# Layer 0's router products of a four-layer adaLN/MoE kernel: a moving operand of 56 columns, 48 of them zeros, in place of 8

## The chip, the cores and the metric

The kernel runs on one core of a Trainium2 chip. The metric is the device time of one execution in microseconds; a profile gives the span from the first to the last instruction of one execution, which is a little shorter.

## The reference

The input is x, 8 sequences of 128 tokens with 128 features. Four layers follow; each takes a conditioning step and then a mixture-of-experts step, and adds the result to x. The change touches the routing of the first conditioning step:

```python
# layer 0, conditioning: D = 128, E = 8 experts, K = 2, N = 8*128 tokens
tf = broadcast(t_emb)                                  # one vector per sequence
shared = silu(xf @ w1) * (xf @ w3) @ w2
s = sigmoid(concat([xf, tf], -1) @ router_W)           # router_W is 256 x 8
topk_idx = top_k(s + router_bias, K)
gates = s[topk_idx] / sum(s[topk_idx])
h = gelu(einsum('nc,ech->enh', xf, W1e))
routed = sum_e combine[n, e] * (h[e] @ W2e[e])
out = (shared + routed) / 3
```

A second mixture (squared ReLU) completes layer 0. Layer 1 has a GRU over 128 steps, layer 2 a low-rank product per sequence, layer 3 a recurrence with tanh; each is followed by a mixture of 8 or 12 experts. All of it is float32, much of it split in two parts of the PE's rounded float32 type.

## The kernel before, in words

The program is written per engine. Each engine has its own instruction stream in which the order is set by hand, and they meet at semaphores. The tokens are cut into four chunks of 256 columns (32 time steps of 8 sequences). The work of the layers is a list of slots, `UNITS`; in slot n TensorE projects unit n into the bank `U` (`project`), ScalarE applies the activation (`hidden`), TensorE multiplies unit n - 2 down into the bank `Y` (`down`), and VectorE adds the weighted result into `acc_a` or `acc_b` (`add_l0`, line 1015 the first one, line 803 the others). Units "C" are layer 0's conditioning step, "F" its mixture. From slot `GRU_SLOT` on the steps of layer 1's GRU are put between them, and later those of layer 3's recurrence.

The start goes like this. GpSimd makes the identity (lines 487 and 488), clears buffers, and makes masks (lines 491 to 511), signalling `zeros` and `consts`; `own` makes GpSimd wait for its own instruction. TensorE multiplies the identity with itself eight times (`keep_busy`, line 1385), turns x eight times into the banks `Y` (line 1394), from where VectorE copies it into `xT` (line 903; the profile calls this buffer `h`), and multiplies twice more. It projects the units of slots 0 and 1 (`l_w`), and then comes `router_c` (line 1398), called in slot 1. It waits for the first loads and for the constants, turns the conditioning input and two small tables into bank M[0], waits until VectorE has laid out the conditioning vectors (`cond_tok`), and makes the router's scores in M[1]: for each of the 8 tiles of 128 tokens, the tile of `xT` is the stationary operand and the 8 columns of `l0_rw` are moved; a ninth product does it for the conditioning. All `mm` calls are recorded at line 1364, and a float32 product stands in the trace as two records.

VectorE takes the scores in `scores_c` (line 924): it copies the ninth product's 8 columns to `okay` and adds them to the 64 of the tiles, into `score`. ScalarE makes the sigmoid (`sigmoid_c`), and `route_c` on VectorE finds the two best experts and the weights `comb_x` of the first chunk at once, in slot 2, and of the rest in slots 4 to 9, between the additions of `add_l0`.

Of the kernel before, what the change touches and what calls it, by code (L numbers as in the profile page):

```python
# [7 lines left out]
ALU = mybir.AluOpType  # L8
# [3 lines left out]
P = 128  # L12
B, T, D = 8, 128, 128
# [4 lines left out]
E = 8  # L18
# [19 lines left out]
L0_UNITS += [("F", i, CHUNKS - 1) for i in range(6)]  # L38
HOLD = 4
MID_SLOT = 7  # L40
REST_C = 4
GRU_SLOT = L0_UNITS.index(("F", 5, 0)) + 5

# [23 lines left out]
def unit(n):  # L67

    return UNITS[n] if 0 <= n < len(UNITS) else ("", 0, 0)
# [50 lines left out]
def x_late(n):  # L120

    names = [("mid", m) for m in range(3) if n == MID_SLOT + m // 2]
    names += [("zp", unit(n - 3)[2])] if unit(n - 3)[:2] == ("A", LU - 1) else []
# [27 lines left out]
def at(start, n):  # L151

    return slice(start, start + n)
# [19 lines left out]
def adaln_ffn_program(nc, a, out):  # L173
    with ExitStack() as ctx:
        def sb(name, shape, dtype=F32, scope=ctx):
            return scope.enter_context(nc.sbuf_tensor(name, shape, dtype))
# [4 lines left out]
        def psum(name):  # L181
            return ctx.enter_context(nc.psum_tensor(name, [P, 512], F32))

        def sem(name):
            return ctx.enter_context(nc.semaphore(name))
# [8 lines left out]
        rows = sb("rows", [1, 3 * E + 1])  # L194
        rnn_b = sb("rnn_b", [D, 1])
        cond = sb("cond", [B, D])
        l0_rw = sb("l0_rw", [P, 2, E])
        b2 = [sb(f"l{l}_b2", [P, D]) for l in (1, 2)]
        gate_w = sb("gate_w", [P, 2, E])
        l2_v = sb("l2_v", [P, B * R])  # L200
# [6 lines left out]
        cond_tok = sb("cond_tok", [D, P])  # L207
# [11 lines left out]
        xT = h3[:, B:]  # L219
# [53 lines left out]
        with ExitStack() as early:  # L273
# [33 lines left out]
        score = sb("score", [P, NG])  # L307
# [16 lines left out]
        okay = sb("okay", [P, E])  # L324
# [11 lines left out]
        M = [psum("M0"), psum("M1")]  # L336
# [12 lines left out]
        m_full, m_free = sem("m_full"), sem("m_free")  # L349
# [25 lines left out]
            (rows[:, E:2 * E], a["L1_ffn_gate_b"].unsqueeze(0)),  # L375
            (rows[:, 2 * E:3 * E], a["L2_ffn_gate_b"].unsqueeze(0)),
            (rows[:, 3 * E:], a["L1_ffn_temperature"].unsqueeze(0)),
            (l0_rw[:, :, :], a["L0_cond_router_W"].rearrange("(h d) e -> d h e", h=2)),
            (l0f_rw_in[:, :], a["L0_ffn_router_w"]),
        ]  # L380
        small_loads = [
# [38 lines left out]
        def bank_of(*name):  # L420

            return M[m_of(*name) % 2]
# [62 lines left out]
        def _(pool):  # L485
            own = OwnOrder(pool, pool_own)
# [2 lines left out]
                               base=0, pattern=[[-1, P]], channel_multiplier=1).then_inc(ident_made, 1)  # L489
            for t in (cond_pair, b2[0], b2[1], l3_b2):  # L490
                pool.memset(t[:, :], 0.0).then_inc(zeros, 1)
            own(pool.memset(rank_mask[:, :], 1.0 / (D * R)))
            own(pool.memset(earlier8[:, :, :], 1.0))
            own(pool.memset(earlier12[:, :, :], 1.0))
# [82 lines left out]
        def _(sc):  # L577
# [14 lines left out]
            def mid_copies(n):  # L592
                if n == MID_SLOT + 1:
                    m = bank_of("mid", 0)
                    sc.wait_ge(m_full, m_of("mid", 0) + 1)
                    nc.scalar.activation(l2_uT[:, :], m[:, 0:P], ACT.Copy)
                    nc.scalar.activation(l2_wT[:, :], m[:, P:2 * P], ACT.Copy).then_inc(m_free, 1)
                if n == MID_SLOT + 2:
                    m = bank_of("mid", 2)
                    sc.wait_ge(m_full, m_of("mid", 2) + 1)  # L600
                    sc.wait_ge(m_free, m_of("mid", 1) + 1)
                    nc.scalar.activation(b1T[:, :], m[:, 0:2 * E * Q], ACT.Copy)
                    nc.scalar.activation(l3_pT[:, :], m[:, 128:128 + DA], ACT.Copy)
                    nc.scalar.activation(l3_uT[:, :], m[0:DA, 256:256 + NR3 * E3], ACT.Copy).then_inc(m_free, 1)
# [149 lines left out]
            def idle(*_):  # L754
                pass
# [34 lines left out]
        def _(dve):  # L790
            own = OwnOrder(dve, dve_own)
            v = nc.vector

            def tt(out, in0, in1, op):
                return v.tensor_tensor(out=out, in0=in0, in1=in1, op=op)  # L795
# [9 lines left out]
            def grp(t, g, n):  # L805
                return t[:, 0:g * n].rearrange("p (g n) -> p g n", g=g)
# [114 lines left out]
            GX = T * B // P  # L921
            SX = GX * E

            def scores_c():
                dve.wait_ge(m_full, M_PRO)
                own(v.tensor_copy(okay[:, :], M[1][:, SX:SX + E]))
                tt(grp(score, GX, E), grp(M[1], GX, E), okay[:, :].unsqueeze(1).to_broadcast([P, GX, E]), ALU.add).then_inc(m_free, 1)

            def route_c(tiles, parts):

# [75 lines left out]
            def add_l0(n, part):  # L1006

                stream, i, k = unit(n)
                if not stream or stream not in "CF" or n not in DOWNS:
                    return  # L1010
                j = DOWNS.index(n)
                if (stream, i) == ("C", 1):
                    if part == 0:
                        dve.wait_ge(y_full, j + 1)
                        v.tensor_copy(acc_a[:, :, :], by_tile(Y[j % 2])).then_inc(y_free, 1)
                        dve.wait_ge(y_free, j + 1)
                elif stream == "C":
                    experts = [(c, t, k * TILES + t, 2 * (i - 2) + e2) for c, e2, t in PAIR]
                    add_expert(j, experts, part, acc_a, comb_x)
                elif i < 2:  # L1020
                    add_expert(j, [(c, t, t, 2 * i + e2) for c, e2, t in PAIR], part, acc_b, comb_f[k % 2], i == 0)
                elif part < TILES:
                    add_expert(j, [(t * D, t, t, 2 + i) for t in range(TILES)], part, acc_b, comb_f[k % 2])
# [5 lines left out]
            def later_set_up():  # L1029
                m = taken("mid", 1)  # L1030
                dve.wait_ge(m_free, m_of("mid", 0) + 1)
                tt(pair_bias[:, 0:3 * D], pair_bias[:, 0:3 * D], m[0:40, 0:3 * D], ALU.add).then_inc(m_free, 1)

            def take_sums(n):

                if n == MID_SLOT + 1:
                    later_set_up()
# [206 lines left out]
            for n in range(A_START):  # L1244
                for quarter in range(4):
# [19 lines left out]
                    if n != 4:  # L1265
                        add_l0(n - 3, quarter)
                    if quarter == 3 and REST_C <= n < REST_C + 6:
                        route_c(range(TILES, GX), (n - REST_C,))
                    if quarter == 3 and n < GRU_SLOT:
# [92 lines left out]
        def _(pe):  # L1362
            def mm(out, lhsT, rhs, start=True, stop=True, shared=False):
                return nc.tensor.matmul(out, lhsT, rhs, start=start, stop=stop, skip_group_check=shared)  # L1364
# [27 lines left out]
            for i in range(2):  # L1392
                for b in range(4):
                    last = nc.tensor.transpose(Y[i][:, b * T:(b + 1) * T], x_in[:, 4 * i + b, :], ident[:, :])
# [3 lines left out]
            def router_c():  # L1398
                pe.wait_ge(ld_first, 16 * FIRST)
                pe.wait_ge(consts, 5)  # L1400
                mm(M[0][:, 0:B], cond[:, :], ident[0:B, 0:B])
                mm(M[0][:, B:B + 3 * E + 1], ones_row[:, 0:P], rows[:, :])
                mm(M[0][:, 64:64 + E], l0f_rw_in[:, :], ident[0:E, 0:E]).then_inc(m_full, 1)
                pe.wait_ge(set_up, 1)
                pe.wait_ge(x_rest, 2)
                for i in range(T * B // P):
                    mm(M[1][:, i * E:(i + 1) * E], xT[:, i * P:(i + 1) * P], l0_rw[:, 0, :])
                last = mm(M[1][:, T * B // P * E:(T * B // P + 1) * E], cond_tok[:, :], l0_rw[:, 1, :])
                last.then_inc(m_full, 1)

            def bank(*name):
# [3 lines left out]
            def later_set_up():  # L1415
                pe.wait_ge(ld_small, 16 * SMALL)
                m = bank("mid", 0)
                nc.tensor.transpose(m[:, 0:P], l2_v[:, :], ident[:, :])
                nc.tensor.transpose(m[:, P:2 * P], l2_w_in[:, :], ident[:, :]).then_inc(m_full, 1)
                m = bank("mid", 1)  # L1420
                pe.wait_ge(set_up, 2)
                mm(m[0:40, 0:3 * D], cond_tok[:, 0:40], gru_c[:, :]).then_inc(m_full, 1)

            def address_set_up():
                m = bank("mid", 2)
                mm(m[:, 0:2 * E * Q], b1_in[:, :], ident[0:2 * E * Q, 0:2 * E * Q])
                mm(m[:, 128:128 + DA], l3_p_in[:, :], ident[0:DA, 0:DA])
                mm(m[0:DA, 256:256 + NR3 * E3], l3_u_in[:, :], ident[0:NR3 * E3, 0:NR3 * E3]).then_inc(m_full, 1)
# [205 lines left out]
            def idle(*_):  # L1634
                pass
# [30 lines left out]
            for n in range(A_START):  # L1666
# [12 lines left out]
                if n == 1:  # L1679
                    router_c()  # L1680
                if n == MID_SLOT:
                    later_set_up()
                if n == MID_SLOT + 1:
                    address_set_up()
# [114 lines left out]
```

## Time and profile before

| | |
|---|---|
| median of 3 runs | 635.3 us (634.16 to 636.39) |
| the profiled execution | 633.13 us |
| its span | 631.4 us |
| mean granted TensorE clock | 0.998 |
| TensorE busy | 607.3 us, 96% of the span |
| VectorE busy | 345.0 us, 55% |
| ScalarE busy | 286.9 us, 45% |
| GpSimd busy | 110.4 us, 17% |

PE is TensorE multiplying, PEld TensorE loading weights, DVE VectorE, ACT ScalarE, POOL GpSimd, SP the engine that issues most loads. Times are from the span's start. Tile names are printed without numbers: `l_rw` is `l0_rw`, `M` either of the banks M[0] and M[1]. In a timeline the number behind x is the count of records merged into the row, the number in brackets the idle time before it and who ended it. The spacing of starts tells more of TensorE than the length of a record, since records overlap.

### The profile page before, as it was taken

How to read it: one execution, taken by the hardware profiler on the slowest of the kernel's cores; microseconds unless marked ns; L12 is line 12 of the kernel's file. 1: busy time of each engine (PE TensorE's matmuls, PEld its weight loads, DVE VectorE, ACT ScalarE, POOL GpSimd, SP SyncE). 2: the span in 40 equal slices, each digit the busy share in tenths (PEclk: the TensorE clock that was granted, in tenths of full speed). 3: DMA queues.
4: the chain of work that ended last, by engine and by line, in shares of the span. 5: the costliest groups of instructions: out<-in, count | busy, mean ns of one | idle time of the engine just before them, and what ended most of it. 6: DMA issues, size and time to landing. Idle time of an engine off the chain costs nothing.

```text
span 631.4 us, 12504 instructions
## 1 busy us (share of the span) xinstructions
PE 607.3 (96%) x4574; PEld 564.7 (89%) x4574; DVE 345.0 (55%) x1205; ACT 286.9 (45%) x955; POOL 110.4 (17%) x325
## 2 busy tenths in 40 slices
PE   8889999999999999999999999998999999999996
PEld 7678788889999999999999999998989889898895
DVE  4875656754464454445554553158747664765514
ACT  3275645645655455444554456545823323311110
POOL 3134111111111111111111110000211221321310
PEclk9999999999999999999999999999999999999999
DMA  8998000000000000000000000091102002002000
GB/s 259 342 300 126 1 1 2 2 2 1 2 2 1 2 1 2 2 2 1 3 1 2 1 2 2 24 178 31 72 2 69 37 5 103 5 6 100 9 1 8
DMA packets 47309, 26.94 MB, mean 43 GB/s; under 512 B 28340, under 2 KB 42512, under 8 KB 46736
## 3 DMA queue, kind: packets, MB, share of 16 engines
q1 hardware_dynamic: 45224, 25.66, 15.1%
q8 instruction: 36, 0.59, 0.4%
q10 hardware_dynamic: 2024, 0.48, 0.4%
q14 instruction: 25, 0.20, 0.1%
HBM read 25.57 MB, written 0.57 MB: 41 GB/s over the span
## 4 chain that ended last, share of the span: by engine, by line
PE 78%; DVE 14%; ACT 3%; issue 3%; DMA 1%; SPq 0%; POOL 0%; DVEq 0%; POOLq 0%
PE Y L1364 30%; PE U L1364 27%; PE HH L1364 7%; PE ZR L1364 7%; PE M L1364 6%; DVE acc_a L803 3%; DVE gated L795 1%; DMA l_bc<-dw 1%; ACT gated L637 1%; DVE rank L835 1%; DVE acc_b L803 1%; DVE rh L803 1%; DVE relu L795 1%; DVE cmp_a L795 0%; DVE fresh L803 0%
## 5 line engine op out<-in xcount | busy, mean ns | idle before, releaser
L1364 PE MATMUL Y<-l_dn,gated 128*128 128x128 f32 x1152 | 162.9, 284 | 1.4 <-DVE acc_a L803 0.7
L1364 PEld LDWEIGHTS Y<-l_dn,gated 128*128 128x128 f32 x1152 | 141.1, 192 | 4.6 <-issue 3.2
L637 ACT ACTIVATE gated<-U,b1T 128x256 f32<-128x256 f32 x256 | 106.6, 473 | 0.0
L1364 PE MATMUL U<-l_x_hi,l_up_hi 128*128 128x256 f32 x256 | 82.8, 324 | 1.0 <-DVE l_x_lo L795 1.0
L619 ACT ACTIVATE h<-ZR,rnn_b 128x8 f32<-128x8 f32 x128 | 34.2, 267 | 95.1 <-PE ZR L1364 92.9
L803 DVE SCALAR_TENSOR_TENSOR fresh<-zr_s,cand 128x8 f32<-128x8 f32 x128 | 21.4, 167 | 95.0 <-ACT cand L615 92.7
L1364 PE MATMUL U<-l_x_lo,l_up_hi 128*128 128x256 f32 x256 | 72.0, 281 | 0.0
L1364 PE MATMUL U<-l_x_hi,l_up_lo 128*128 128x256 f32 x256 | 72.0, 281 | 0.0
L539 POOL TENSOR_SCALAR zh<-zr_s 128x8 f32<-128x8 f32 x128 | 25.7, 201 | 255.4 <-ACT zr_s L611 255.4
L615 ACT ACTIVATE cand<-HH 128x8 f32<-128x8 f32 x128 | 22.7, 177 | 96.3 <-PE HH L1364 96.3
L1364 PE MATMUL U<-scaled_hi,l_up_hi 128*128 128x256 f32 x192 | 58.1, 302 | 1.4 <-POOL scaled_lo L555 1.4
L1364 PE MATMUL U<-scaled_hi,l_up_lo 128*128 128x256 f32 x192 | 54.4, 283 | 0.0
L1364 PE MATMUL U<-scaled_lo,l_up_hi 128*128 128x256 f32 x192 | 54.3, 283 | 0.0
L1364 PEld LDWEIGHTS HH<-rh,gru_u 128*128 128x128 f32 x256 | 39.2, 189 | 13.6 <-DVE rh L803 12.4
L1364 PEld LDWEIGHTS U<-l_x_hi,l_up_hi 128*128 128x128 f32 x256 | 48.8, 191 | 1.7 <-DVE l_x_lo L795 1.1
L1364 PEld LDWEIGHTS U<-l_x_hi,l_up_lo 128*128 128x128 f32 x256 | 48.8, 191 | 0.0
L1364 PEld LDWEIGHTS U<-l_x_lo,l_up_hi 128*128 128x128 f32 x256 | 48.3, 189 | 0.0
L803 DVE SCALAR_TENSOR_TENSOR acc_a<-Y,mix,acc_a 128x128 f32<-128x128 f32 x96 | 33.6, 350 | 25.9 <-PE Y L1364 23.4
L1364 PEld LDWEIGHTS ZR<-h,rnn_w 128*128 128x128 f32 x256 | 41.0, 190 | 7.4 <-ACT h L619 5.1
L1364 PE MATMUL ZR<-h_gru,gru_u 128*128 128x8 f32 x256 | 47.1, 257 | 0.0
L1364 PE MATMUL HH<-rh,gru_u 128*128 128x8 f32 x256 | 40.4, 230 | 5.2 <-DVE rh L803 4.4
L1364 PEld LDWEIGHTS HH<-h_gru,gru_u 128*128 128x128 f32 x256 | 39.5, 191 | 4.6 <-DVE h_gru L803 3.6
(263 smaller groups left out, 1207.7 us busy)
## 6 DMA issues: line engine op xcount, KB each, us to landing
l_bc<-dw SPq DMA_DIRECT2D x4, 1536.0 KB, 6.4
stage<-L_ffn_W_dram SPq DMA_DIRECT2D x4, 768.0 KB, 10.4
w_raw<-L_ffn_W_dram SPq DMA_DIRECT2D x12, 256.0 KB, 7.0
l_up_raw<-L_ffn_W_dram SPq DMA_DIRECT2D x1, 2048.0 KB, 9.6
l_up_raw<-L_ffn_w_dram SPq DMA_DIRECT2D x1, 2048.0 KB, 14.6
l0f_up<-L_ffn_w_dram SPq DMA_DIRECT2D x1, 768.0 KB, 7.2
l0f_dn<-L_ffn_w_dram SPq DMA_DIRECT2D x1, 768.0 KB, 8.7
x<-x_dram SPq DMA_DIRECT2D x1, 512.0 KB, 4.4
```

Of the source, the lines that this page charges most:

```text
L539: own(nc.gpsimd.tensor_scalar(zh[:, :], zr_s[:, 0, :], -0.5, 0.5, ALU.mult, ALU.add))
L615: nc.scalar.activation(cand[:, :], HH[:, at(N + step % CT * B, B)], ACT.Tanh).then_inc(gru_cand, 1)
L619: nc.scalar.activation(h3[:, at((step + 1) * B, B)], ZR[:, at(step % CT * B, B)], ACT.Tanh, bias=rnn_b[:, 0:1]).then_inc(rnn_h, 1)
L637: last = nc.scalar.activation(gated[:, n % 4, h * N:(h + 1) * N], U[n % 2][:, h * N:(h + 1) * N], ACT.Gelu, bias=b1T[:, col:col + 1])
L795: return v.tensor_tensor(out=out, in0=in0, in1=in1, op=op)
L803: return v.scalar_tensor_tensor(out=out, in0=in0, scalar=scalar, in1=in1, op0=op0, op1=op1)
L835: own(v.tensor_reduce(out=grp(rank, g, n), in_=ca, axis=AX.X, op=ALU.add))
L1364: return nc.tensor.matmul(out, lhsT, rhs, start=start, stop=stop, skip_group_check=shared)
```

## The change

`l0_rw` grows from 8 to 56 columns for each of its two halves. The weights are loaded into the first 8; GpSimd sets the other 48 to zero in one more instruction, behind the memsets of `b2` and ahead of `rank_mask`, and waits for it. The nine router products move all 56 columns, and their results lie 56 columns apart in M[1] (9 x 56 = 504 of 512). VectorE reads the first 8 of each group. No instruction changes its place on TensorE, VectorE, ScalarE or the load queue.

```diff
+WIDE_RW = 56
...
-        l0_rw = sb("l0_rw", [P, 2, E])
+        l0_rw = sb("l0_rw", [P, 2, WIDE_RW])
...
-            (l0_rw[:, :, :], a["L0_cond_router_W"].rearrange("(h d) e -> d h e", h=2)),
+            (l0_rw[:, :, 0:E], a["L0_cond_router_W"].rearrange("(h d) e -> d h e", h=2)),
...
             for t in (cond_pair, b2[0], b2[1], l3_b2):
                 pool.memset(t[:, :], 0.0).then_inc(zeros, 1)
+            own(pool.memset(l0_rw[:, :, E:], 0.0))
             own(pool.memset(rank_mask[:, :], 1.0 / (D * R)))
...
             def scores_c():
                 dve.wait_ge(m_full, M_PRO)
-                own(v.tensor_copy(okay[:, :], M[1][:, SX:SX + E]))
-                tt(grp(score, GX, E), grp(M[1], GX, E), okay[:, :].unsqueeze(1).to_broadcast([P, GX, E]), ALU.add).then_inc(m_free, 1)
+                own(v.tensor_copy(okay[:, :], M[1][:, at(GX * WIDE_RW, E)]))
+                tt(grp(score, GX, E), grp(M[1], GX, WIDE_RW)[:, :, 0:E], okay[:, :].unsqueeze(1).to_broadcast([P, GX, E]), ALU.add).then_inc(m_free, 1)
...
                 for i in range(T * B // P):
-                    mm(M[1][:, i * E:(i + 1) * E], xT[:, i * P:(i + 1) * P], l0_rw[:, 0, :])
-                last = mm(M[1][:, T * B // P * E:(T * B // P + 1) * E], cond_tok[:, :], l0_rw[:, 1, :])
+                    mm(M[1][:, at(i * WIDE_RW, WIDE_RW)], xT[:, i * P:(i + 1) * P], l0_rw[:, 0, :])
+                last = mm(M[1][:, at(T * B // P * WIDE_RW, WIDE_RW)], cond_tok[:, :], l0_rw[:, 1, :])
                 last.then_inc(m_full, 1)
```

## Rows read from the trace of the kernel before

**Rows 1.** Page: busy us, share of the span, instructions, of each engine.

```profile
PE 607.3 (96%) x4574; PEld 564.7 (89%) x4574; DVE 345.0 (55%) x1205; ACT 286.9 (45%) x955; POOL 110.4 (17%) x325
```

**Rows 2.** Page: the chain that ended last, shares by engine.

```profile
PE 78%; DVE 14%; ACT 3%; issue 3%; DMA 1%; SPq 0%; POOL 0%; DVEq 0%; POOLq 0%
```

**Rows 3.** Timeline of TensorE from 0: start us, us, instructions, count of records.

```profile
1.58 3.78 PE L1364 MATMUL HH<-ident 128*128 128x128 f32 x16 [1.58 <-POOL ident L488]
5.25 1.97 PE L1394 MATMUL Y<-ident,x 128*128 128x128 f32 x8
7.01 0.88 PE L1364 MATMUL HH<-ident 128*128 128x128 f32 x4
7.80 1.97 PE L1364 MATMUL U<-h,l_w 128*128 128x256 f32 x8
9.69 0.39 PE L1364 MATMUL M<-ident,cond 8*128 8x8 f32 x2
...
11.04 1.95 PE L1364 MATMUL M<-l_rw,h 128*128 128x8 f32 x16 [0.52 <-DVE cond_tok L913]
12.85 0.37 PE L1364 MATMUL M<-l_rw,cond_tok 128*128 128x8 f32 x2
13.07 1.97 PE L1364 MATMUL U<-h,l_up 128*128 128x256 f32 x8
...
16.90 1.05 PE L1364 MATMUL Y<-l_dn,gated 128*128 128x128 f32 x8
17.79 1.03 PE L1364 MATMUL U<-h,l_up 128*128 128x256 f32 x4
18.66 1.05 PE L1364 MATMUL Y<-l_dn,gated 128*128 128x128 f32 x8
```

**Rows 4.** Timeline of VectorE, the same columns.

```profile
6.41 0.40 DVE L903 COPY h<-Y 128x128 f32<-128x128 f32 x1 [6.41 <-PE Y L1394]
...
13.26 0.17 DVE L926 COPY okay<-M 128x8 f32<-128x8 f32 x1 [0.30 <-PE M L1364]
13.46 0.23 DVE L795 TENSOR_TENSOR score<-M,okay 128x64 f32<-128x64 f32 x1
...
16.05 0.42 DVE L1015 COPY acc_a<-Y 128x256 f32<-128x256 f32 x1
```

**Rows 5.** The chain in order of time: start us, us, engine, tile, line.

```profile
11.04 2.19 PE M L1364 x18
...
29.12 0.53 DVE acc_a L803 x2
29.70 0.44 PE M L1380 x2
```

**Rows 6.** Tile `l_rw`: count, ns min/median/max, first and last start.

```profile
L1364 PEld LDWEIGHTS M<-l_rw,h x16: 186/192/193, 11.0 to 12.7; 128*128 128x128 f32 x16
...
L1364 PE MATMUL M<-l_rw,cond_tok x2: 257/257/257, 12.8 to 13.0; 128*128 128x8 f32 x2
```

**Rows 7.** Timeline of TensorE, one 128-column record with its length.

```profile
24.23 0.27 PE L1418 MATMUL M<-ident,l_v 128*128 128x128 f32 x1
```

**Rows 8.** Timeline of GpSimd, the same columns.

```profile
2.21 0.15 POOL L493 MEMSET earlier<- 128x64 f32 x1
2.42 0.22 POOL L494 MEMSET earlier<- 128x144 f32 x1
2.69 0.30 POOL L495 MEMSET ones_row<- 1x256 f32 x1
...
6.19 0.63 POOL L511 TENSOR_SCALAR_AFFINE_SELECT earlier<-earlier 128x64 f32<-128x64 f32 x2
```

**Rows 9.** Stretches of 4 us: busy of each engine, then PEclk, DMA share, GB/s.

```profile
8.00:12.00 4.00, 3.48 (x23) 2.90 (x22) 2.37 (x9) 0.95 (x2) 0.00 (x0) 1.00 1.09 364
...
28.00:32.00 4.00, 2.46 (x14) 1.82 (x14) 2.45 (x9) 0.83 (x5) 2.56 (x4) 1.00 1.01 299
...
628.00:632.00 4.00, 0.00 (x0) 0.00 (x0) 0.12 (x1) 0.00 (x0) 0.00 (x0) 0.60 0.07 16
```

## The prediction

> **What bounds the kernel now.** I read the busy table first [rows 1]: TensorE multiplies for 96% of the span, VectorE works for 55%, and no other engine is near. The chain that ended last [rows 2] says the same: 78% of it is TensorE, 14% VectorE. So over the whole kernel a microsecond counts if it is TensorE's, or if TensorE waits for it. The change touches neither the weight products nor the recurrence that fill the span, only a piece of about 2 us near its start, so I went on to that piece.
>
> TensorE's timeline there [rows 3] shows the router products from 11.04 to about 13.1 us. Each float32 product is two records, so the 8 token tiles are 16 records and the conditioning product is 2. Behind them VectorE waits, 0.30 us for the last product [rows 4]; then it adds the scores, ScalarE takes the sigmoid, and VectorE ranks, masks and normalises. The chain in order of time [rows 5] runs through exactly these pieces: TensorE's 18 router records from 11.04, then the score addition, the sigmoid and VectorE's routing and additions up to 29.12, and TensorE's turning of `acc_a` at 29.70. A delay of the router's end is therefore not hidden. It moves VectorE's whole chain, and TensorE with it, by its own length. The reader should keep both facts: the place is on the path, and the place is short.
>
> **The change part by part.**
>
> *Wider moving operand, 18 records.* What do 48 more columns cost a record? The spacing of starts in [rows 3] tells. At 8 columns 16 records go from 11.04 to 12.85, 0.113 us each. At 128 columns 8 records go from 16.90 to 17.79, 0.111 us each. At 256 columns 4 records go from 17.79 to 18.66, 0.218 us each. So 8 and 128 columns have the same spacing, and only beyond 128 does it grow. Something that does not depend on the columns sets the pace at both; the weight load is the candidate, since each record loads its own 128x128 weights for 0.192 us [rows 6], partly beside the one before. 56 columns lie between two widths that cost the same, so I take 18 x 0 = 0. Both ends: below, a gain of 18 x 0.002 = 0.04 us (the difference of 0.113 and 0.111); above, the 256-column spacing, 18 x (0.218 - 0.113) = 1.9 us. The row at 128 is by far the nearer.
>
> *End of the last record.* A record alone lasts 0.257 us at 8 columns [rows 6] and 0.272 us at 128 columns [rows 7]. 48 of those 120 columns more give 0.015 x 48/120 = 0.006 us, and I take 0.01 us. This lies on the path, because VectorE's copy of the conditioning scores waits for it.
>
> *VectorE reads the scores from groups 56 apart.* `scores_c` still copies 8 values and adds 64, in two instructions of 0.17 and 0.23 us [rows 4]. The same elements are read, in groups of 8 with a gap of 48. The nearest row for scattered reading is the copy of x out of a bank, which takes 0.40 us for 128 elements, against 0.42 us for 256 elements in a row [rows 4]. By it a scattered element may cost up to twice a packed one. For 64 elements that is between 0 and 0.13 us (64 x 0.40/128 = 0.20, less 64 x 0.42/256 = 0.105, rounded up for the second operand). The new groups are the same 8 elements long as the old ones, so I take 0.01 us.
>
> *The memset of the 48 columns.* GpSimd clears 2 x 48 = 96 elements per partition and waits for itself. Its neighbours of 64 and 144 elements start 0.21 and 0.27 us before the next instruction [rows 8], so everything behind it on GpSimd moves by about 0.25 us. What is behind it are the constants: the last of them ends at 6.82 us. TensorE first asks for them at 9.69 us, ahead of the conditioning transpose, and VectorE later still. The cover is 9.69 - 6.82 = 2.9 us, ten times the delay; if it were gone, the price would be 0.25 us. The memset comes behind the identity, with which TensorE starts at 1.58, and behind the four memsets that the sync queue waits for, so neither moves.
>
> *The load.* The router weights come in pieces of 8 numbers from DRAM before and after; only the place they land in is spread. TensorE did not stand for a load ahead of the products of 9.69 or 11.04 [rows 3]: no idle time is noted at the one, and VectorE ends the 0.52 us at the other. Cost 0. Later buffers move up by 384 bytes a partition; nothing in the trace prices that, and I take 0.
>
> Sum: 0 + 0.01 + 0.01 + 0 = +0.02 us, between -0.04 and +2.1 us (1.9 + 0.015 + 0.13). The profiled execution took 633.13 us and would take 633.15. It stands 2.2 us under the median of the runs, 635.3; the same difference put on the median gives **635.3 us**.
>
> **The rivals.**
>
> *Rival 1: the clock falls in some executions, and the change holds it up.* Of the clock this trace shows three things. First, the records of the 8 products that only keep TensorE busy start 0.229 us apart (1.58 to 5.25, [rows 3]), twice the 0.111 of the same width later. So TensorE ran at the lower of its two levels, 1.2 GHz, although the column of the granted clock says 1.00 there. The four such records ahead of the projections are still 0.198 us apart (7.01 to 7.80) and the projections behind only 0.236, near the 0.218 of their width, so the clock rose at about 7.6 us. Second, after that the column is 1.00 in every stretch, through the router, and through 28 to 32 us, where TensorE is busy for only 2.46 of 4 us. Third, it falls to 0.50 at the end, some 2 us after the last product [rows 9]. In the profiled execution the clock did not fall at the router, and there the change can give back nothing. But the stretch from 9.69 to 13.1 is the thinnest in columns of the start: three small transposes, a wait of 0.52 us, and 18 records of 8 columns. If the chip counts columns moved and not instructions, some executions could lose the clock there. The price from rows: the low stretch at the start lasted 6.0 us, and a second one as long would cost at most half of it, 3.0 us, since VectorE waits for TensorE's products at 16.05 and behind. The timed runs lie 1.0 to 3.3 us above the profiled one, which such a fall could explain, and so could the moment at which the clock rises first. If the median run has the fall and loses it, the time is that of the profiled execution, about **633.2 us**, 0.33% less; if every run had it in full, 632.3.
>
> The Trainium skill ("TensorE: Matmul & The Clock Gate", section on the HAM clock gate) says that the low clock is the default and that activity releases it. It does not say whether a product of 8 columns counts as activity. The low start agrees with it, and no fall at the router is seen here. By that rule the change helps where 8 columns count as idle, which is this rival. For it: 56 columns keep the array moving for seven times as long at no cost in spacing. Against it: the one trace there is shows nothing to hold up. Chance 0.24.
>
> *Rival 2: the columns are not hidden.* If moving adds to loading below 128 columns too, the slope from 128 to 256 applies: (0.218 - 0.111)/128 = 0.84 ns a column. 48 columns make 0.040 us a record, and 18 records 0.7 us on the path. The place is TensorE from 11.04 to 13.1, and the result is **636.0 us**, slower by 0.1%. It decides as soon as the spacing leaves 0.113 us. At the far end, the 256-column spacing and scattered reads at twice the price, it is 637.4, slower by 0.3%. Against it stand the equal spacings of 8 and 128 columns. Chance 0.10.
>
> *Rival 3: the change does nothing.* Zero columns or cheap ones may not count for the clock either. The time is then the forecast's, and it cannot be told from it by the time alone.
>
> **How the numbers follow.** A measurement of this kernel can tell about 0.3%, 1.9 us, from no change; three runs of before alone spread over 2.2 us. Forecast and rival 3 together, no change of note: 0.66, of which scatter puts 0.03 on each side. Rival 1: 0.24, of which 0.15 ends beyond 0.3% and 0.09 within. Rival 2: 0.10, of which 0.05 beyond and 0.05 within. Faster: 0.15 + 0.03 = 0.18; slower: 0.05 + 0.03 = 0.08; same: 0.74. The range goes down to 632.9, which takes in most of rival 1, and up to 636.9, which takes in rival 2 at its own price and the highest run of before (636.39).
>
> **What would show it.** In the changed profile, 16 router records with starts 0.11 us apart, a last record of some 0.26 us, a score addition of 0.23 to 0.25 us, the memset at 2.1 us with the constants done by 7.1, and the granted clock at 1.00 through 7.6 to 30 us as before. Spacing near 0.15 us shows rival 2. A median near 633 us with no difference inside two undisturbed traces, or a changed kernel whose runs lie closer together, speaks for rival 1. The prediction is wrong if the median leaves 632.9 to 636.9, or if the router's stretch changes by more than 0.2 us.

## The result, and the profile after

| | before | changed |
|---|---|---|
| median | 634.16 us (5 runs) | 639.28 us (5 runs) |
| ratio | | 1.0069, 95% interval 1.0049 to 1.009 |
| profiled execution | 633.13 us | 637.19 us |
| its span | 631.4 us | 635.4 us |
| mean granted clock of the profiled execution | 0.998 | 0.994 |

The changed kernel is slower by 0.7%, or by 0.4% in the larger comparison below (e1). Ratios leave disturbed executions out (two of the changed kernel's five, 651.8 and 655.1 us), so they are not the quotient of the medians. The forecast was 635.3 us, between 632.9 and 636.9. It named a slower kernel only through products that are not hidden, and that is not where the time went.

The router first. This is the timeline of TensorE in the changed kernel, with the columns of [rows 3]:

```profile
10.64 1.99 PE L1366 MATMUL M<-l_rw,h 128*128 128x56 f32 x16 [0.52 <-DVE cond_tok L915]
12.47 0.39 PE L1366 MATMUL M<-l_rw,cond_tok 128*128 128x56 f32 x2
12.69 1.95 PE L1366 MATMUL U<-h,l_up 128*128 128x256 f32 x8
...
29.31 0.44 PE L1382 MATMUL M<-ident,acc_a 128*128 128x128 f32 x2 [0.49 <-DVE acc_a L805]
29.59 1.06 PE L1366 MATMUL Y<-l_w,gated 128*128 128x128 f32 x8
34.78 2.05 PE L1366 MATMUL U<-l_in,l0f_up 128*128 128x256 f32 x4 [4.14 <-issue]
36.62 0.86 PE L1366 MATMUL M<-l0f_rw,l_in 128*128 128x8 f32 x4
37.34 2.06 PE L1366 MATMUL Y<-l_dn,gated 128*128 128x128 f32 x8
39.18 1.72 PE L1366 MATMUL U<-l_in,l0f_up 128*128 128x256 f32 x4
40.74 1.05 PE L1366 MATMUL Y<-l_dn,gated 128*128 128x128 f32 x8
```

The 16 wide records start (12.47 - 10.64)/16 = 0.114 us apart; the narrow ones took 0.113 [rows 3]. From the first router record to the next projection it is 2.05 us now and was 2.03. The router's products together cost 0.02 us more. At 29.31 us the changed kernel is even 0.39 us ahead of the one before [rows 5], a lead that it has since the first copies of x and so before any router product.

The time goes behind that. These are the rows of TensorE before for the same places:

```profile
29.97 1.06 PE L1364 MATMUL Y<-l_w,gated 128*128 128x128 f32 x8
32.72 1.10 PE L1364 MATMUL U<-l_in,l0f_up 128*128 128x256 f32 x4 [1.69 <-issue]
...
35.86 1.05 PE L1364 MATMUL Y<-l_dn,gated 128*128 128x128 f32 x8
```

TensorE stood for 4.14 us in place of 1.69, and started 2.06 us later instead of 0.39 earlier. Then its products took almost twice as long: from 34.78 to 40.74 it is 5.96 us, before 3.14. Together the changed kernel is 4.88 us behind at 40.74. It gets back 1 us at VectorE's next stand, and about 4 us stay to the end: the spans differ by 4.0 us. The stretches show the clock that was granted (busy of each engine, PEclk, DMA share, GB/s), before:

```profile
32.00:36.00 4.00, 3.29 (x22) 3.05 (x23) 3.67 (x8) 3.12 (x8) 2.86 (x3) 1.00 1.03 392
36.00:40.00 4.00, 4.00 (x30) 3.61 (x29) 3.69 (x14) 3.36 (x7) 0.00 (x0) 1.00 1.04 386
```

and changed:

```profile
32.00:36.00 4.00, 1.22 (x3) 1.07 (x4) 1.68 (x4) 1.93 (x6) 1.84 (x2) 0.72 1.00 342
36.00:40.00 4.00, 4.00 (x16) 3.68 (x16) 1.92 (x5) 2.62 (x4) 0.68 (x1) 0.50 1.05 345
```

In the 4.14 us without a product the granted clock fell to 0.50, the 1.2 GHz level, and between 36 and 40 us TensorE got through 16 records where it had got through 30. Who held TensorE? The profile says "issue", which means that it shows no one for whom TensorE waited. ScalarE's timeline of the changed kernel leads to the answer:

```profile
26.10 0.60 ACT L633 ACTIVATE gated<-U 128x512 f32<-128x512 f32 x1 [1.38 <-PE U L1366]
33.24 0.63 ACT L684 ACTIVATE l_up_hi<-l_up_raw 128x512 fp32r<-128x512 f32 x1 [6.54 <-DMA l_dn<-L_ffn_W_dram]
33.78 0.20 ACT L604 ACTIVATE b1T<-M 128x64 f32<-128x64 f32 x1
33.88 0.21 ACT L605 ACTIVATE l_pT<-M 128x64 f32<-128x64 f32 x1
33.98 0.18 ACT L606 ACTIVATE l_uT<-M 64x36 f32<-64x36 f32 x1
```

followed by VectorE's wait for the last of these copies (waited for, us in total, times, longest):

```profile
DVE l_in L801 <- ACT l_uT L606: 4.1, 1, 4.1
```

and ScalarE before:

```profile
31.17 0.63 ACT L682 ACTIVATE l_up_hi<-l_up_raw 128x512 fp32r<-128x512 f32 x1 [4.09 <-DMA l_dn<-L_ffn_W_dram]
```

In slot 8 ScalarE rounds the first expert of layer 1's up weights (`up_high`), and waits for both loads of `ld_l1`, the up weights and `l1_dn`, although it reads only the first. ScalarE got it 2.07 us later in the changed kernel (33.24 in place of 31.17). Behind it on ScalarE stand the copies `b1T`, `l3_pT` and `l3_uT`; VectorE's `l_in` waits for the last of them, and TensorE multiplies `l_in`. The change touches none of this. But the loads are slower. The first line gives a queue's packets, MB and share of the 16 DMA engines, the second the us from the issue of `l1_dn` to its landing (the 0.5 KB is what the view prints; by its shape the load has 2 MB). Before:

```profile
q1 hardware_dynamic: 45224, 25.66, 15.1%
...
l_dn<-L_ffn_W_dram SPq DMA_DIRECT2D x1, 0.5 KB, 10.0
```

and changed:

```profile
q1 hardware_dynamic: 45224, 25.66, 15.8%
...
l_dn<-L_ffn_W_dram SPq DMA_DIRECT2D x1, 0.5 KB, 11.2
```

The same number of packets and the same bytes took 15.8% of 635.4 us in place of 15.1% of 631.4 us, 5% more of the engines' time. `l1_dn` took 1.2 us longer from issue to landing, and it was issued 0.87 us later (at 21.99 in place of 21.12 us), behind the other loads of its queue. What could slow the loads of a kernel in which no load has changed its size or its order? One thing did change for all of them: with `l0_rw` 384 bytes longer, every buffer behind it lies 384 bytes higher in its partition.

### The profile page after: what moved, and what is told of

The parts are those of the page before. It is cut to its first block, busy times and chain, and to the rows that moved or that the text cites. A ratio compares the mean times of both kernels' runs of the same rounds, so it can differ in the third digit from the quotient of the medians.

```text
span 635.4 us, 12505 instructions
## 1 busy us (share of the span) xinstructions
PE 609.6 (96%) x4574; PEld 566.6 (89%) x4574; DVE 344.2 (54%) x1205; ACT 287.1 (45%) x955; POOL 110.5 (17%) x326
## 3 DMA queue, kind: packets, MB, share of 16 engines
q1 hardware_dynamic: 45224, 25.66, 15.8%
## 4 chain that ended last, share of the span: by engine, by line
PE 78%; DVE 13%; ACT 3%; issue 3%; DMA 1%; SPq 0%; POOL 0%; DVEq 0%; POOLq 0%
PE Y L1366 30%; PE U L1366 27%; PE HH L1366 7%; PE ZR L1366 7%; PE M L1366 6%; DVE acc_a L805 3%; DVE gated L797 1%; DMA l_bc<-dw 1%; ACT gated L639 1%; DVE rank L837 1%; DVE acc_b L805 1%; DVE rh L805 1%; DVE relu L797 1%; DVE fresh L805 0%; ACT cand L617 0%
```

## The experiments

In the first four runs the parts of the change stand apart: the placement, the wide products and the memset. **e1**, the changed kernel once more:

> The changed kernel once more, beside the kernel before. In its profile TensorE waited 4.14 us ahead of the first l0f_up product instead of 1.69 us, because ScalarE waited 6.54 us for the load of l1_dn (4.09 us before), and TensorE's clock then fell to 0.5 for 6.8 us. Theory A (the loads' speed differs with the placement of the buffers, 384 bytes a partition): again 637 to 640 us. Theory B (the loads are slower or faster from execution to execution, whatever the kernel; the five runs fell badly): the two kernels within 0.3% of each other, both with a spread of several us. Theory C (wider products themselves): again 637 to 640.

Measured: 637.46 us median of 12, ratio 1.0038 (1.0016 to 1.006). The result stands, though a bit smaller. ScalarE waited 5.3 us for `l1_dn`, TensorE 2.9 us, and the clock was down again behind it (0.50 over 36 to 40 us). Here it was down at the router too (0.63 over 12 to 16 us), so that TensorE turned `acc_a` at 30.85 us, 1.54 later than in the first profile; but it started on `l_in` at 35.08, only 0.30 later, and both executions took about 637.2 us. In the changed kernel `l1_dn` sets the time at this point, and what was lost ahead of it was hidden in the wait.

**e2**, the placement alone:

```diff
         l0_rw = sb("l0_rw", [P, 2, E])
+        sb("pad_rw", [P, 2, 48])
```

> The kernel before with an unused buffer of 2 x 48 columns behind l0_rw, so that everything behind it lies 384 bytes higher in each partition, as after the change; products of 8 columns, no memset. Theory A (placement): slow as the changed kernel, 637 to 640 us. Theory B (executions scatter) and theory C (wide products): as the kernel before, 634 to 636.

Measured: 637.64 us, ratio 1.0045 (1.0016 to 1.0074). A buffer that nobody reads or writes makes as large a loss as the whole change in e1. **e3**, the other way round:

```diff
-        l0_rw = sb("l0_rw", [P, 2, WIDE_RW])
+        sb("old_rw", [P, 2, E])
...
         sb("room", [P, 64])
+        l0_rw = sb("l0_rw", [P, 2, WIDE_RW])
```

> The changed kernel with the 56-column buffer allocated behind all others, and a buffer of the old size left in the old place, so that all other buffers lie where they lay before; wide products, memset and strided reading stay. Theory A (placement): 634 to 636 us, as before. Theory C (wide products): 637 to 640. Theory B: no difference from before.

Measured: 634.15 us, ratio 0.9998 (0.9977 to 1.0019). Wide products, memset and scattered reading are all in, only the shift is not, and the loss is gone. The loads, of e2:

```profile
q1 hardware_dynamic: 45224, 25.66, 15.9%
```

and of e3:

```profile
q1 hardware_dynamic: 45224, 25.66, 14.8%
...
l_dn<-L_ffn_W_dram SPq DMA_DIRECT2D x1, 0.5 KB, 9.6
```

**e4**, the memset alone, on a buffer at the end:

```diff
         sb("room", [P, 64])
+        spare = sb("spare", [P, 2, 48])
...
+            own(pool.memset(spare[:, :, :], 0.0))
             own(pool.memset(rank_mask[:, :], 1.0 / (D * R)))
```

> The kernel before with one more GpSimd memset of 96 elements a partition, on a spare buffer at the end, and the wait for it, so that the constants and all that is behind on GpSimd come 0.24 us later. Nothing hangs on it by the trace: every theory expects 634 to 636 us, within 0.3% of before. If it is slow, the shift of GpSimd's memsets against the first loads is the cause.

Measured: 633.8 us, ratio 0.9992 (0.997 to 1.0014). It costs nothing that can be told, as forecast.

So theory A holds, and B and C fall. What about the placement matters? Counted from the sizes of the buffers, `l1_dn` begins at byte 161280 of a partition before and at 161664 after, the one a multiple of 256 and 512, the other 128 past a multiple of 256. No view of the profile prints an address, and the count hangs on where the first buffer lies; what the runs themselves show is the effect of each shift. The targets of the other large weight loads have the same remainders, since the buffers between are multiples of 512 long. **e5** and **e6** shift by less, with `sb("pad_rw", [P, 32])` and `sb("pad_rw", [P, 64])` in the place of e2's buffer:

> The kernel before with an unused buffer of 32 columns (128 bytes a partition) behind l0_rw. l1_dn then begins at byte 161408 of a partition, 128 past a multiple of 256; before it is 161280, a multiple of 256 and 512, and in the changed kernel 161664, 128 past a multiple of 256. Theory A1 (only where the loads' targets lie against multiples of 256 bytes matters): slow as the changed kernel, 637 to 638 us, l1_dn landing later than 32 us. Theory A2 (multiples of 512): slow too. Theory A3 (the distance of 384 bytes itself, or the larger total): as before, 634, or between.

Measured: 637.68 us, ratio 1.0059 (1.0031 to 1.0086).

> The same with 64 columns, 256 bytes: l1_dn begins at 161536, a multiple of 256 but not of 512. Theory A1: as before, 633.5 to 634.5 us. Theory A2: slow, 637 to 638. [...]

Measured: 634.3 us, ratio 1.0004 (0.9983 to 1.0026). The larger of the two shifts costs nothing and the smaller all of it, which leaves theory A1: of the shifts 0, 128, 256 and 384 bytes, those that leave a remainder of 128 modulo 256 are slow. Other remainders were not tried. The loads of e5:

```profile
q1 hardware_dynamic: 45224, 25.66, 15.8%
```

and of e6:

```profile
q1 hardware_dynamic: 45224, 25.66, 14.9%
```

and the stands of ScalarE and TensorE (waited for, us in total, times, longest), in e5:

```profile
ACT l_up_hi L683 <- DMA l_dn<-L_ffn_W_dram: 4.5, 1, 4.5
...
PE U L1365 <- issue: 2.1, 1, 2.1
```

and in e6, where TensorE no longer stands:

```profile
ACT l_up_hi L683 <- DMA l_dn<-L_ffn_W_dram: 1.7, 1, 1.7
```

The stand of e5 is only 2.1 us, and the clock went down there too (0.50 over 36 to 40 us). The share of q1 divides all profiles of the study without overlap: 14.8 to 15.1% in the nine whose loads begin on a multiple of 256 (before, e3, e4, e6, e7 and e9 to e12), and 15.8 to 15.9% in the five whose loads begin 128 past one (changed, e1, e2, e5, e8). Packet by packet the traces say it more sharply: the 4096 packets of 2048 bytes took 90 to 93 ns each on average in the nine, and 103 to 106 ns in the five. The Trainium skill ("DMA: Bandwidth & Descriptors", section on how a descriptor splits into AXI transactions) has a rule for this: a transaction must start from an address aligned to 256 bytes, so a descriptor that begins elsewhere has its first transaction start at the boundary below, and the bytes ahead of its own start, fetched and not used, still cost beats of the bus. These runs agree in direction. The size of the loss, 5 to 8% more of the engines' time, is the runs'; that this rule is the reason is argued and not shown.

The next two ask how slower loads turn into time. In **e7** (on the kernel before) and **e8** (on the changed one) the up weights get a semaphore of their own:

```diff
-        ld_w13 = sem("ld_w13")
+        ld_w13, ld_l1_up = sem("ld_w13"), sem("ld_l1_up")
...
-            sp.dma_start(l1_up_raw[:, :, :], a["L1_ffn_W1"].rearrange("e d f -> d e f")).then_inc(ld_l1, 16)
+            sp.dma_start(l1_up_raw[:, :, :], a["L1_ffn_W1"].rearrange("e d f -> d e f")).then_inc(ld_l1_up, 16)
...
-                        sc.wait_ge((ld_l1, ld_l2)[l], 16 * L12_LOADS)
+                        sc.wait_ge(*((ld_l1_up, 16), (ld_l2, 16 * L12_LOADS))[l])
...
-                        pe.wait_ge((ld_l1, ld_l2)[stream == "B"], 16 * L12_LOADS)
+                        pe.wait_ge(*((ld_l1, 16), (ld_l2, 16 * L12_LOADS))[stream == "B"])
```

> The kernel before, with l1_up_raw on a semaphore of its own: ScalarE's first copy of layer 1's up weights (l1_up_hi, slot 8) waits for l1_up_raw alone and no longer for l1_dn, which TensorE needs only in layer 1. Theory (the late l1_dn holds ScalarE, which holds the copies behind it, so VectorE's l_in and TensorE): TensorE's wait of 1.7 us ahead of the first l0f_up product goes, 632 to 633 us. Rival (the next wait is right behind it, on l1_up_raw or on GpSimd): 634.

Measured: 634.04 us, ratio 0.9987 (0.997 to 1.0003). TensorE's stand is gone, but no gain can be told. The expected 1.7 us came from one execution, in which the clock had held at the router. In e4 and e6, whose loads are placed the same way modulo 256, the clock was down there, TensorE turned `acc_a` at 30.67 and 31.26 us instead of 29.70, and the stand was 0.3 us or none. The rival's next wait was not seen at TensorE either, though its 634 us was met.

> The same edit on the changed kernel. If the slower loads cost time only through ScalarE's wait for l1_dn and the fall of TensorE's clock behind it, the 2.4 us between the two kernels go and this comes to 632 to 633.5 us, as e7. If the loads are late elsewhere too (stage, l2_dn, or the first ones), 634 to 636.

Measured: 632.83 us, ratio 0.9986 (0.9963 to 1.001). The loads are as slow as in the changed kernel:

```profile
q1 hardware_dynamic: 45224, 25.66, 15.9%
...
l_dn<-L_ffn_W_dram SPq DMA_DIRECT2D x1, 0.5 KB, 11.8
```

and yet nothing is lost that can be told from the kernel before. ScalarE rounds at 27.80 us without a stand, and TensorE starts on `l_in` at 31.97. (The profiled execution of e8 took 636.9 us, but its clock was down at the router, at 56 us and at 440 us; e3, whose loads are fast, had the same three falls and took 636.92.) So the slow loads cost time through this one wait: ScalarE for `l1_dn`, and behind it TensorE's stand and clock. The runs don't separate the last two.

The last four ask whether the 56 columns do anything for the clock (rival 1). **e9** is e3 with the edit of e7, **e10** is e7 again beside it. **e11** is e10, and **e12** is e9, with one more edit, three identity products on TensorE just ahead of the router's:

```diff
+                keep_busy(3)
                 pe.wait_ge(set_up, 1)
                 pe.wait_ge(x_rest, 2)
```

> All of the change's wide products, with the buffer at the end (loads aligned as before) and l1_up_raw on its own semaphore. Beside e10 it tells what the 56 columns themselves do. Theory (they do nothing for the clock): as e10, 633.5 to 634.5 us. Rival 1 of the prediction (they keep the clock from falling at the router in more executions): a median nearer to the undisturbed 631 to 632 us.

> The kernel before with l1_up_raw on its own semaphore, once more, as the partner of e9 and e11 on the same chip: 633.5 to 634.5 us, with the granted clock at 0.5 for some 3 us at the router in most executions.

> As e10, with three more identity products (keep_busy, 6 records, 0.67 us by their spacing of 0.111) in TensorE's wait of 0.5 us for cond_tok, just ahead of the 8-column router products. If the thin stretch at the router is what makes the clock fall there, it falls in fewer executions: a median of 632 to 633 us. If it falls for another reason, 634 to 634.5 us, since the products lengthen the stretch by up to 0.2 us.

> e9 and e11 together: if activity in columns decides, the fewest falls at the router of the four, 631.5 to 632.5 us, faster than both kernels of the study. If neither matters, 634.

| | columns | keep_busy(3) | median | ratio to before | mean clock at least 0.995, of the executions in the ratio |
|---|---|---|---|---|---|
| e9 | 56 | no | 634.13 us | 0.9986 (0.996 to 1.0012) | 4 of 9 |
| e10 | 8 | no | 634.10 us | 1.0002 (0.9983 to 1.0021) | 2 of 11 |
| e11 | 8 | yes | 634.14 us | 1.0007 (0.9982 to 1.0033) | 3 of 12 |
| e12 | 56 | yes | 632.07 us | 0.9972 (0.9954 to 0.9991) | 7 of 12 |

Neither edit alone moves the median. Both together are 0.3% faster than before, the only kernel of the study that beats it clear of the interval. The interval of e12 overlaps the others', so that both are needed is not shown.

Counted by execution, the medians hide something. With the loads' wait out of the way (e7 to e12), 15 of 32 executions with 56 columns have a mean clock of 0.998 or more (5 of 11 in e8, 4 of 9 in e9, 6 of 12 in e12), and 4 of 33 with 8 columns (0 of 10 in e7, 1 of 11 in e10, 3 of 12 in e11); in the kernel before, run beside them, it is 7 of 60. The products of `keep_busy` make less of a difference in the same count: 9 of 24 with them, 10 of 41 without. So the wide products may well hold the clock in more executions, in fewer than half of them, which hardly moves a median. The count was made after the fact, and e3 (56 columns, 1 of 11) does not show it, so it is a hint and not a result.

The clock does fall at the router. In e10 (8 columns; stretches as above):

```profile
12.00:16.00 4.00, 4.00 (x19) 3.47 (x19) 2.88 (x10) 3.51 (x5) 0.00 (x0) 0.69 1.15 329
...
436.00:440.00 4.00, 4.00 (x22) 3.42 (x23) 3.19 (x7) 1.78 (x5) 0.00 (x0) 0.60 0.04 7
```

and it falls with 56 columns too, in e3:

```profile
12.00:16.00 4.00, 4.00 (x15) 3.35 (x15) 2.41 (x10) 3.00 (x4) 0.00 (x0) 0.57 1.15 326
```

The second row of e10 shows a second fall, far behind the router, which the profiles of e4, e7, e9 and e12 have as well. In e12 the clock held at the router, and fell in the stretch at 30 us and again at 436 us:

```profile
12.00:16.00 4.00, 3.80 (x26) 3.44 (x25) 2.62 (x11) 3.91 (x5) 0.00 (x0) 1.00 1.15 332
28.00:32.00 4.00, 3.49 (x16) 2.95 (x17) 3.76 (x12) 1.41 (x5) 2.62 (x4) 0.76 0.91 300
32.00:36.00 4.00, 4.00 (x25) 3.63 (x24) 1.88 (x7) 2.53 (x5) 2.86 (x3) 0.82 1.01 348
...
436.00:440.00 4.00, 4.00 (x23) 3.42 (x22) 2.98 (x6) 1.78 (x5) 0.00 (x0) 0.57 0.18 37
```

## Why the prediction was wrong

**The step that failed** is the last of "The load": "Later buffers move up by 384 bytes a partition; nothing in the trace prices that, and I take 0." No bound stands beside that 0. e2 shows that this shift alone makes the kernel slower by 0.45% (2.9 us), as much as the whole change in e1 (0.38%, 2.4 us) within the intervals, and e3 and e6 show that without it, or with another shift, nothing is lost. The trace of the kernel before had no price for slower loads, but it showed that they would not be hidden: ScalarE already stood 4.09 us for `l1_dn`, and TensorE 1.69 us behind it, so in that execution each microsecond by which `l1_dn` comes later is one on the path. With the 5% that the runs have since shown, what lands by 31 us would come about 1.5 us later (an estimate, 31 x 0.05; ScalarE's start moved by 2.07), and the low clock adds to it: 2.82 us in the changed profile (5.96 - 3.14).

**What bounds the kernel.** The chain at the start was read as VectorE's up to 29.70, and nothing was read behind it. TensorE's next stand, 1.69 us of "issue" ahead of 32.72, was the weak place. The sentence that TensorE "did not stand for a load" was true of the router's and not asked of the others.

**The wide products** were right: 0.114 us of spacing where 0.113 was forecast, and rival 2 (0.15) did not come. The last record takes 0.275 us, not 0.26, against 0.257 before, so that term was 0.02 where 0.01 was taken (it had been interpolated towards 0.272 us at 128 columns, which 56 already reach). **The reading in groups 56 apart** was right. The score addition took 0.23 us before; in VectorE's timeline of the changed kernel it is:

```profile
13.09 0.22 DVE L797 TENSOR_TENSOR score<-M,okay 128x64 f32<-128x64 f32 x1
```

**The memset** was right: 0.17 us, what is behind it on GpSimd 0.24 us later (the 64-element memset at 2.45 in place of 2.21), and no effect in e4.

**Rival 1** had its mechanism in part. The clock does fall at the router in most profiled executions: in 11 of the 14 profiles the granted clock of 12 to 16 us is 0.57 to 0.74. The profile of before, that of the changed kernel and e12's are the three at 1.00, so the trace that I argued from was an exception. The price of one fall was forecast at no more than 3.0 us, and it is less than half of that. In e10 the one execution with a mean clock of 0.999 took 631.68 us and those with 0.994 about 634.1, but these 2.4 us are the price of two falls, as the profile of e10 shows; e6, whose profile has only the one at the router, took 632.84, 1.2 us more than 631.68 (two kernels, one execution each, so an estimate). And 56 columns do not prevent the fall in every execution (e3, e8 and e9 have it). In the changed kernel the gain could not have come in any case: there `l1_dn` sets the time behind the router, as e1 shows.

**Rival 2** named the right side for the wrong reason, and its upper end (637.4) came near the time by accident (637.46 in e1).

## What to carry to other kernels

A buffer's length is also the placement of all buffers behind it: keep the targets of large loads on multiples of 256 bytes, or put a new odd-sized buffer last. Ask of a change which waits for loads are already open, since those turn any slowing of the loads into time; and give a load that is needed early a semaphore of its own. A stand of TensorE can cost its clock as well: in the changed kernel 2.45 us more of standing (4.14 against 1.69) were followed by 2.82 us lost at the low clock. And count the falls of the clock in a profile before pricing one of them.

## What the runs showed of the hardware

The loads into SBUF take 5 to 8% more of the DMA engines' time when most of them begin 128 bytes past a multiple of 256 of a partition, at equal packets and bytes (15.8 to 15.9% of the span against 14.8 to 15.1%; 103 to 106 ns against 90 to 93 ns for a packet of 2048 bytes); a start at a multiple of 256 that is not one of 512 is as good as one of 512 (e6, 14.9%). A 56-column float32 record of TensorE starts as fast behind another as an 8-column one, 0.114 and 0.113 us, and ends 0.018 us later (0.275 and 0.257). The granted clock went to 0.50 during or right behind stands of TensorE of 4.14 us (changed), 2.91 us (e1) and 2.14 us (e5), and stayed at 1.00 over one of 1.69 us (before). It differs from execution to execution of the same kernel, and most of the scatter between 631 and 637 us goes with it: in e12 the six executions at 0.998 and 0.999 lie between 630.75 and 631.37 us, those at 0.993 and 0.994 between 633.02 and 634.37. Why it holds at the router in some executions and not in others, and which of e12's two edits does how much, stays open.
